# Self attention inside a decoder layer: another order of the same work on GpSimd, VectorE, TensorE, ScalarE and the DMA queue

## The chip, the cores and the metric

The kernel runs on one core of one Trainium2 chip. The metric is the device time of one execution in microseconds (us): TensorE (PE), VectorE (DVE), ScalarE (ACT), GpSimd (POOL) and SyncE (SP), which issues the DMAs of this stage, run their own instruction streams and meet at semaphores.

## The reference, cut to what matters

```
x: (32, 100, 512) float32, 16 heads of 32; ctx: (32, 722, 512)
q, k, v = x@Wq, x@Wk, x@Wv
R_hat   = (1 + exp(v)) / (1 + exp(v - w*|i-j|))           # one 100 x 100 table for each head
scores  = relu(q k^T) * R_hat, causal mask, / sqrt(32)
attn    = softmax(scores);   ctx = attn @ v
x = layernorm(x + ctx @ Wo + bo)
x = layernorm(x + cross_attention(x, ctx_1024))
x = layernorm(x + gated_feed_forward(x))
```

Only the self attention (q, k, v, scores, softmax, attn @ v) is touched. What it computes stays the same.

## The kernel before

The program has three stages in time: self attention (about 0 to 400 us of the trace), a short stage that projects its output, normalises it and projects the queries of the cross attention (400 to 580 us), and cross attention with the feed forward (580 us to the end).

The self attention walks over the 32 batch items b in **steps** s. Two kinds of work are interleaved in a step.

- **Units.** A unit (line 798) is one tile of x@Wq, x@Wk or x@Wv: 12 matmuls, of 320 columns for q and k, of 512 for v. There are 21 for each group of 640 tokens, 105 in all; 11 run ahead of step 0, and each of the first 28 steps holds 3 or 4. In a step they sit in four slots: one unit in each of slots 0, 1 and 2, and the fourth, where there is one, in slot 3. ScalarE takes each from PSUM (`take_unit`, line 528; three PSUM buffers), SP stores it to HBM (`store_unit`), and SP loads q, k and v of item b back as [head dimension, token] tiles (`load_qk`, line 297; `load_v`, line 304).
- **The softmax of one item**, spread over four steps. `scores(b)` (line 821, TensorE) fills one PSUM area; `scale(b)` (655, VectorE) multiplies it with the table into e; `maximum(b, half)` (663) takes row maxima of 8 heads; `exps(b, half)` (541, ScalarE) are eight exponentials with their sums; `invert_sums(b, half)` (670, VectorE) takes 1/sum; `normalise(b, half)` (448, GpSimd) multiplies: the "products"; `turn_blocks(b, half)` (675, VectorE) transposes 32 x 32 blocks of e into the one buffer `turned`. The blocks off the diagonal go from `turned` to `pT` by six DMAs (`move(b)`, line 310, SP), the four on it by four copies (`copy_diagonal(b)`, line 454, GpSimd). `weighted_sum(b)` (831, TensorE) multiplies pT with v, `take_result(b)` (550, ScalarE) takes it from PSUM and `store_o(b)` (322, SP) stores it.

Each engine does its instructions in the order in which they are written; nothing is reordered at run time. `turned` and `pT` are single buffers: `turn_blocks(b)` waits until `move(b-1)` has landed and `copy_diagonal(b-1)` is done, and both of these wait for `weighted_sum(b-1)`. e, q, k, rowsum and the output tile have two buffers or two halves.

In step s, with c = s-1 and b = s-2, the order before is

- TensorE: unit, weighted_sum(s-3), unit, scores(s), unit, and the fourth unit;
- ScalarE: exps(c, 0), unit, exps(c, 1), unit, take_result(s-3), the other units;
- VectorE: scale(c), maximum(c, 0), turn(b, 0), maximum(c, 1), turn(b, 1), invert_sums(c, 0), invert_sums(c, 1);
- GpSimd: products of (c, 0), of (c, 1), copies of b, and in 12 of the steps one eighth of a later token group is split into a high and a low part (`split_x`);
- SP: stores of units, load_qk(s), load_v(s-1), in three steps a load of x, move(s-2), store_o(s-4).

The wait that ties GpSimd's copies to products of the next item stands in `copy_diagonal`:

```
pool.wait_ge(turn_done, 2 * (b + 1))
wait(pool, pv_done, b)
pool.wait_ge(norm_done, 2 * min(b + 2, B))
```

From step 29 on there are no units. There, TensorE does filler matmuls (`between`, line 869), VectorE and ScalarE split the next weights (`c_low`, `c_high`; lines 109 and 103), and the next stage begins on VectorE with `low_o` behind the last `turn_blocks`.

Of the kernel before, what the change touches and what calls it, by code (L numbers as in the profile page):

```python
# [12 lines left out]
KD = D // P  # L13
# [110 lines left out]
def phase_self_attention(nc, sem, passed, xT, wq, wk, wv, w, v, q_d, k_d, v_d, o_d, x, bo, bq, x1_d, cq_d, raws, cross_w,  # L124
# [20 lines left out]
    with ExitStack() as ctx, ExitStack() as of_attention, ExitStack() as of_units, ExitStack() as of_outputs:  # L145
# [123 lines left out]
        with nc.Block() as block:  # L269
# [4 lines left out]
            def _(sp):  # L274
# [3 lines left out]
                def load_x(g):  # L278
                    sp.wait_ge(x_low, 1 + KD * (g - 1))
                    if g == 1:  # L280
                        sp.wait_ge(first_low, KD)
                    sp.dma_start(xraw[:, :, :], x_cols[:, :, col(g * GT, GT)]).then_inc(x_loaded, 16)
# [39 lines left out]
                def store_o(b):  # L322
                    sp.wait_ge(o_done, b + 1)
                    sp.dma_start(tiled[2][:, :, col(b * T, T)], oo[b % 2][:, :, :]).then_inc(o_stored[b % 2], 16)
# [56 lines left out]
                for s in range(B + 3):  # L381
                    while stored < units_before(s):
                        store_unit(stored)
                        stored += 1
                    if s < B:
                        load_qk(s)
                    if 1 <= s < B + 1:
                        load_v(s - 1)
                    if s in (2, 8, 14):
                        load_x((s + 4) // 6 + 1)  # L390
                    if 2 <= s < B + 2:
                        move(s - 2)
                    if s >= 4:
                        store_o(s - 4)
                    if s == LAST_UNITS + 1:
                        sp.wait_ge(unit_done, TOTAL)
                        for which in range(2):
                            for h in range(2):
                                sp.wait_ge(qk_stored[which][h], 16 * NG)
                        for i in range(V_RING):  # L400
                            sp.wait_ge(v_stored[i], 16 * ((TT * NG - i + V_RING - 1) // V_RING))
                        sp.sem_inc(a_freed, 1)
                        load_o(0)
                        load_x1(0)
                        sp.dma_start(bo_b[:, :], bo.rearrange("(a n) -> a n", a=1).broadcast_to([P, D]))\
                          .then_inc(b_loaded, 16)
                        sp.dma_start(bq_c[:, :], bq).then_inc(b_loaded, 16)
# [24 lines left out]
            def _(pool):  # L432
# [6 lines left out]
                def split_x(g, k):  # L439
                    if k == 0:  # L440
                        wait(pool, unit_done, UNITS * (g - 1))
                        pool.wait_ge(x_loaded, 16 * g)
                    pool.tensor_copy(xs[g % 2][0][:, k, :], xraw[:, k, :]).then_inc(x_high, 1)
                    pool.wait_ge(x_high, 2 + KD * (g - 1) + k)
                    pool.tensor_tensor(xs[g % 2][1][:, k, :], xraw[:, k, :], xs[g % 2][0][:, k, :].bitcast(F32),
                                       ALU.subtract).then_inc(x_low, 1)
# [4 lines left out]
                    pool.tensor_tensor(part, part, inv[:, half, :].unsqueeze(2).broadcast_to([T, HH, T]), ALU.mult)\  # L451
                        .then_inc(norm_done, 1)

                def copy_diagonal(b):
                    pool.wait_ge(turn_done, 2 * (b + 1))
                    wait(pool, pv_done, b)

                    pool.wait_ge(norm_done, 2 * min(b + 2, B))
                    for a in range(BLOCKS):
                        rows = slice(32 * a, 32 * (a + 1))  # L460
                        pool.tensor_copy(pT[rows, a, :, :], turned[rows, a, :, :]).then_inc(diag_done, 1)
                    pool.wait_ge(diag_done, BLOCKS * (b + 1))
# [16 lines left out]
                for tile in e:  # L479
# [3 lines left out]
                pool.affine_select(out=rhat[:, :, :], in_=rhat[:, :, :], compare_op=ALU.is_ge, fill=-MASK,  # L483
                                   base=0, pattern=[[0, H], [-1, T]], channel_multiplier=1).then_inc(rhat_done, 1)
                pool.wait_ge(cleared, 3)
                for s in range(1, B + 2):
                    if s <= B:
                        normalise(s - 1, 0)
                        normalise(s - 1, 1)
                    if s >= 2:  # L490
                        copy_diagonal(s - 2)
                    for g in range(2, NG):
                        if 0 <= s - (6 * g - 8) < KD:
                            split_x(g, s - (6 * g - 8))
                pool.wait_ge(b_loaded, 32)
                for g in range(NG):
                    add_bias(g, 0)
# [11 lines left out]
            def _(act):  # L509
# [72 lines left out]
                for s in range(B + 3):  # L582
                    b, c = s - 3, s - 1
                    for i in range(4):
                        if 0 <= c < B and i < 2:
                            exps(c, i)
                        for u in slot(s, i):
                            take_unit(u)
                        if b >= 0 and i == 1:
                            take_result(b)  # L590
                    if s == B - 2:
                        act.wait_ge(a_freed, 1)
                        act.wait_ge(next_loaded, 80)
                        c_high(act, [0])
                    if s == B - 1:
                        for i in range(TT):
                            high_o(0, i)
                    if s == B:
                        c_high(act, [1])
# [14 lines left out]
            def _(dve):  # L614
# [55 lines left out]
                def invert_sums(b, half):  # L670
                    dve.wait_ge(exp_done, H * b + HH * (half + 1))
                    wait(dve, norm_done, 2 * (b - 1) + half + 1)
                    dve.reciprocal(inv[:, half, :], rowsum[:, half, :]).then_inc(inv_done, 1)
# [90 lines left out]
                for s in range(1, B + 2):  # L764
                    b, c = s - 2, s - 1
                    if c < B:
                        scale(c)
                    for half in range(2):
                        if c < B:
                            maximum(c, half)  # L770
                        if b >= 0:
                            turn_blocks(b, half)
                    if c < B:
                        invert_sums(c, 0)
                        invert_sums(c, 1)
                    if s == B - 1:
                        dve.wait_ge(a_freed, 1)
                        dve.wait_ge(next_loaded, 80)
                        c_low(dve, [0])
# [17 lines left out]
            def _(pe):  # L797
# [85 lines left out]
                for s in range(B + 2):  # L883
                    for i in range(4):
                        for u in slot(s, i):
                            unit(u)
                        if s > LAST_UNITS:
                            between(s, i)
                        if i == 0 and s >= 3:
                            weighted_sum(s - 3)  # L890
                        if i == 1 and s < B:
                            scores(s)
                project_o(0, 2)
                weighted_sum(B - 1)
# [1052 lines left out]
```

## Time and profile before

| | us |
|---|---|
| median of 3 runs | 2523.39 (2519.21 to 2528.76) |
| the profiled execution: its own time | 2524.59 |
| the profiled execution: span | 2522.7 |
| mean granted TensorE clock | 0.975 of full speed |
| busy share of the span: PE / DVE / ACT / POOL | 95% / 61% / 53% / 52% |

The busy shares are those of the whole span. In the self attention no engine is busy all the time, and its 400 us have to be read by themselves: by the table of stretches for how full each engine is, and by the order of instructions in time on each engine, with what ended the idle time ahead of each. PE is busy 95% of the span because the cross attention, three quarters of it, fills PE.

### The profile page before, as it was taken

How to read it: one execution, taken by the hardware profiler on the slowest of the kernel's cores; microseconds unless marked ns; L12 is line 12 of the kernel's file. 1: busy time of each engine (PE TensorE's matmuls, PEld its weight loads, DVE VectorE, ACT ScalarE, POOL GpSimd, SP SyncE). 2: the span in 40 equal slices, each digit the busy share in tenths (PEclk: the TensorE clock that was granted, in tenths of full speed). 3: DMA queues.
4: the chain of work that ended last, by engine and by line, in shares of the span. 5: the costliest groups of instructions: out<-in, count | busy, mean ns of one | idle time of the engine just before them, and what ended most of it. 6: DMA issues, size and time to landing. Idle time of an engine off the chain costs nothing.

```text
span 2522.7 us, 58691 instructions
## 1 busy us (share of the span) xinstructions
PE 2396.4 (95%) x21728; PEld 2067.0 (82%) x21728; DVE 1548.0 (61%) x2625; ACT 1326.0 (53%) x3287; POOL 1312.8 (52%) x1125
## 2 busy tenths in 40 slices
PE   7889876997999999999999999999999899999999
PEld 6777744887888888888888888888888688998998
DVE  7556556873766666676666666766666725344342
ACT  4777662213666666666666666666666652321311
POOL 4666545323666656666665656666665523333322
PEclk9999977998999999999999999999999999999999
DMA  6667664743767777777677777776776861011010
GB/s 201 181 195 199 173 188 150 269 155 93 191 180 189 191 187 194 188 190 187 182 190 187 187 191 192 189 186 182 191 188 179 229 187 64 30 34 54 8 38 22
DMA packets 268845, 404.21 MB, mean 160 GB/s; under 512 B 126236, under 2 KB 143644, under 8 KB 268572
## 3 DMA queue, kind: packets, MB, share of 16 engines
q1 hardware_dynamic: 243996, 350.25, 49.0%
q10 hardware_dynamic: 24576, 50.36, 8.3%
q8 instruction: 165, 2.70, 0.5%
q14 instruction: 108, 0.88, 0.1%
HBM read 134.11 MB, written 52.43 MB: 74 GB/s over the span
## 4 chain that ended last, share of the span: by engine, by line
PE 73%; DVE 1%; DMA 1%; SPq 1%; issue 1%; POOL 0%; ACT 0%; POOLq 0%; DVEq 0%; ACTq 0%
PE D_ps_p L68 41%; PE D_ps_s L1748 7%; PE D_ps_p L1774 6%; PE E_ps_u L68 5%; PE E_ps_g L68 5%; PE E_ps_d L68 5%; PE E_ps_y L68 3%; SPq L1198 1%; DMA E_w_int<-in_w_gate 0%; DMA E_x_last<-x 0%; PE E_ps_t L1801 0%; DVE D_neg_max L1557 0%; DVE D_turned L1571 0%; DMA D_values<-in_ctxT 0%; ACT D_e L1421 0%
## 5 line engine op out<-in xcount | busy, mean ns | idle before, releaser
L1305 POOL TENSOR_SCALAR D_e<-D_e,D_inv 128x722 f32<-128x722 f32 x256 | 538.9, 2105 | 538.4 <-DVE D_inv L1563 538.4
L1421 ACT ACTIVATE D_e<-D_ps_s,D_neg_max 128x723 f32<-128x723 f32 x512 | 438.1, 862 | 409.0 <-DVE D_neg_max L1557 358.4
L1557 DVE TENSOR_REDUCE D_neg_max<-D_ps_s 128x1 f32<-128x723 f32 x512 | 439.7, 900 | 313.1 <-PE D_ps_s L1748 312.9
L1571 DVE STREAM_TRANSPOSE D_turned<-D_e 128x768 f32<-128x768 f32 x512 | 496.3, 972 | 7.1 <-DMA D_pT<-D_turned 4.4
L68 PE MATMUL D_ps_p<-D_ctx_high,cross_wk_high 128*128 128x362 f32 (+1 forms) x1024 | 351.0, 343 | 12.4 <-DVE D_ctx_low L1588 12.4
L68 PE MATMUL D_ps_p<-D_ctx_low,cross_wk_high 128*128 128x362 f32 (+1 forms) x1024 | 337.3, 329 | 0.0
L68 PE MATMUL D_ps_p<-D_ctx_high,cross_wk_low 128*128 128x362 f32 (+1 forms) x1024 | 335.9, 328 | 0.0
L68 PE MATMUL D_ps_p<-cross_wv_high,D_ctx_high 128*128 128x512 f32 (+1 forms) x768 | 303.9, 396 | 0.0
L68 PE MATMUL D_ps_p<-cross_wv_high,D_ctx_low 128*128 128x512 f32 (+1 forms) x768 | 303.3, 395 | 0.0
L68 PE MATMUL D_ps_p<-cross_wv_low,D_ctx_high 128*128 128x512 f32 (+1 forms) x768 | 301.7, 393 | 0.0
L1428 ACT ACTIVATE D_e<-D_e,D_inv 128x722 f32<-128x722 f32 x256 | 230.9, 902 | 8.4 <-DVE D_inv L1563 8.4
L68 PEld LDWEIGHTS D_ps_p<-D_ctx_high,cross_wk_high 128*128 128x128 f32 x1024 | 193.3, 189 | 35.1 <-issue 32.3
L547 ACT ACTIVATE A_e<-A_e,A_neg_max 100x100 f32<-100x100 f32 x512 | 185.9, 366 | 51.2 <-DVE A_neg_max L667 50.9
L1320 POOL TENSOR_TENSOR D_ctx_low<-D_craw,D_ctx_high 128x722 fp32r<-128x722 f32 x124 | 198.9, 1604 | 17.4 <-issue 6.9
L1349 POOL TENSOR_TENSOR E_hidden_low<-E_gated,E_hidden_high 128x320 fp32r<-128x320 f32 x120 | 105.4, 880 | 188.6 <-ACT E_hidden_high L1487 188.6
L68 PEld LDWEIGHTS D_ps_p<-D_ctx_low,cross_wk_high 128*128 128x128 f32 x1024 | 194.1, 190 | 2.7
L1748 PE MATMUL D_ps_s<-D_keys,D_queries 32*128 32x241 f32 (+1 forms) x3072 | 193.6, 380 | 2.6 <-ACT D_e L1421 2.6
L68 PEld LDWEIGHTS D_ps_p<-D_ctx_high,cross_wk_low 128*128 128x128 f32 x1024 | 193.8, 189 | 0.0
L1668 DVE SCALAR_TENSOR_TENSOR E_gated<-E_ps_u,E_gated 128x320 f32<-128x320 f32 x120 | 59.0, 492 | 215.2 <-ACT E_gated L1494 215.2
L1748 PEld LDWEIGHTS D_ps_s<-D_keys,D_queries 32*128 32x128 f32 x3072 | 135.1, 185 | 60.8 <-issue 50.5
L68 PEld LDWEIGHTS D_ps_p<-cross_wv_high,D_ctx_low 128*128 128x128 f32 (+1 forms) x768 | 139.1, 181 | 39.6
L1416 ACT ACTIVATE D_values<-D_ps_p 128x512 f32<-128x512 f32 x192 | 114.4, 596 | 106.8 <-PE D_ps_p L68 106.5
(215 smaller groups left out, 5128.0 us busy)
## 6 DMA issues: line engine op xcount, KB each, us to landing
D_pT<-D_turned SPq DMA_DIRECT2D x1536, 96.0 KB, 2.8
D_pT<-D_turned ACTq DMA_DIRECT2D x512, 96.0 KB, 2.9
D_craw<-in_ctxT SPq DMA_DIRECT2D x126, 361.0 KB, 3.8
A_pT<-A_turned SPq DMA_DIRECT2D x192, 64.0 KB, 2.0
self_q<-A_q_out SPq DMA_DIRECT2D x10, 640.0 KB, 3.9
self_k<-A_k_out SPq DMA_DIRECT2D x10, 640.0 KB, 3.9
self_v<-A_v_out SPq DMA_DIRECT2D x25, 256.0 KB, 3.9
A_q<-self_q SPq DMA_DIRECT2D x32, 200.0 KB, 3.9
```

The source lines that it names most:

```text
L68: last = pe.matmul(out, lhs(a, k), rhs(b, k), start=(k == 0 and n == 0), stop=(k == chunks - 1 and n == len(terms) - 1))
L547: act.activation(head, head, ACT.Exp, bias=neg_max[:, b % 2, h:h + 1], accum_out=rowsum[:, half, i:i + 1]).then_inc(exp_done, 1)
L1305: pool.tensor_scalar(head, head, inv[:, 2 * (s % 2):2 * (s % 2) + 1], None, ALU.mult)\
L1320: pool.tensor_tensor(cs[b % 2][1][:, k, :], craw[k % 2][:, :], cs[b % 2][0][:, k, :].bitcast(F32), ALU.subtract).then_inc(c_low, 1)
L1349: pool.tensor_tensor(hs[1][:, c, cols], gated[u % 2][:, :], hs[0][:, c, cols].bitcast(F32), ALU.subtract).then_inc(hl_done, 1)
L1416: act.activation(vs[b % 2][0:rows, i, :], bank("v", b, i)[0:rows, 0:D], ACT.Copy).then_inc(v_done, 1)
L1421: act.activation(e[n // 2 % 2][:, n % 2, 0:PARTS * PART].rearrange("p (a c) -> p a c", a=PARTS), parts_of(n), ACT.Exp, bias=neg_max[:, n % ...
L1428: act.activation(head, head, ACT.Copy, scale=inv[:, 2 * (s % 2) + 1:2 * (s % 2) + 2])\
L1557: dve.tensor_reduce(neg_max[:, n % 4:n % 4 + 1], parts_of(n), AX.XY, ALU.max, negate=True)\
L1571: dve.transpose(turned[quad % 2][:, :, 2 * (s % 2) + h, :].rearrange("p j (t r) -> p t j r", r=32), e[s % 2][:, h, :].rearrange("p (t j r) ...
L1748: return pe.matmul(of_head[:, j, a, 0:end - first], qs[rows, m, :, :].rearrange("p a q -> p (a q)"), ks[rows, m, first:end], start=True, s ...
L1774: last = pe.matmul(out[HD * j:HD * (j + 1), 0:T], vs[b % 2][:, i, c:c + HD], pT[quad % 2][:, :, j, 32 * i:32 * i + QB], start=(i == 0), st ...
```

## The change

Nothing is added but one wait, and nothing removed but the reach of another; instructions change places.

- GpSimd: the four copies of item b now stand ahead of the products of item c = b+1, not behind them; they no longer wait for these products, and wait in addition for those parts of x that GpSimd itself split before (`x_low`, its own finished work).
- VectorE: invert_sums(b, 1) moves from the end of a step to behind the scale of the next one.
- TensorE: weighted_sum and scores each stand one unit later in a step.
- ScalarE: take_result stands behind the unit of slot 2.
- SP: store_o(s-4) stands ahead of move(s-2), not behind it.

```
                     if s in (2, 8, 14):
                         load_x((s + 4) // 6 + 1)
+                    if s >= 4:
+                        store_o(s - 4)
                     if 2 <= s < B + 2:
                         move(s - 2)
-                    if s >= 4:
-                        store_o(s - 4)
...
-                def copy_diagonal(b):
+                def copy_diagonal(b, splits):
                     pool.wait_ge(turn_done, 2 * (b + 1))
                     wait(pool, pv_done, b)
-                    pool.wait_ge(norm_done, 2 * min(b + 2, B))
+                    pool.wait_ge(norm_done, 2 * (b + 1))
+                    pool.wait_ge(x_low, splits)
...
+                splits = 1 + KD
                 for s in range(1, B + 2):
+                    if s >= 2:
+                        copy_diagonal(s - 2, splits)
                     if s <= B:
                         normalise(s - 1, 0)
                         normalise(s - 1, 1)
-                    if s >= 2:
-                        copy_diagonal(s - 2)
                     for g in range(2, NG):
                         if 0 <= s - (6 * g - 8) < KD:
                             split_x(g, s - (6 * g - 8))
+                            splits += 1
...
-                        if b >= 0 and i == 1:
+                        if b >= 0 and i == 2:
                             take_result(b)
...
                     if c < B:
                         scale(c)
+                    if b >= 0:
+                        invert_sums(b, 1)
                     for half in range(2):
...
                     if c < B:
                         invert_sums(c, 0)
-                        invert_sums(c, 1)
...
-                        if i == 0 and s >= 3:
+                        if i == 1 and s >= 3:
                             weighted_sum(s - 3)
-                        if i == 1 and s < B:
+                        if i == 2 and s < B:
                             scores(s)
```

GpSimd in steps 3 and 4. A_e0 and A_e1 are the two buffers of e (items 2 and 3 here), L451 the product of one half, L461 (L462 in the changed kernel) the copies. Before:

```order
L451 TENSOR_TENSOR A_e0<-A_e0,A_inv 100x8x100 [waits A_inv_done,A_diag_done]
L451 TENSOR_TENSOR A_e0<-A_e0,A_inv 100x8x100 [waits A_inv_done]
L461 COPY A_pT<-A_turned 32x512 [waits A_norm_done,A_pv_done,A_turn_done]
L461 COPY A_pT<-A_turned 32x512 x3
L451 TENSOR_TENSOR A_e1<-A_e1,A_inv 100x8x100 [waits A_inv_done,A_diag_done]
```

and now:

```order
L462 COPY A_pT<-A_turned 32x512 [waits A_norm_done,A_x_low,A_pv_done,A_turn_done]
L462 COPY A_pT<-A_turned 32x512 x3
L451 TENSOR_TENSOR A_e0<-A_e0,A_inv 100x8x100 [waits A_inv_done,A_diag_done]
L451 TENSOR_TENSOR A_e0<-A_e0,A_inv 100x8x100 [waits A_inv_done]
L462 COPY A_pT<-A_turned 32x512 [waits A_norm_done,A_x_low,A_pv_done,A_turn_done]
```

The copies of item 1 moved from behind to ahead of both products of item 2.

VectorE in step 3 and at the start of step 4 (L658/L661 is the scale, L667/L670 a maximum, L679/L682 a turn, L673/L676 an inversion). Before:

```order
L658 SCALAR_TENSOR_TENSOR A_e0<-A_ps_s,A_rhat 100x16x100 [waits A_turn_done,A_s_done]
L667 TENSOR_REDUCE A_neg_max<-A_e0 100x8 [waits A_exp_done,A_rel_done]
L679 STREAM_TRANSPOSE A_turned<-A_e1 128x8x4x32 [waits A_diag_done,A_moved,A_norm_done]
L667 TENSOR_REDUCE A_neg_max<-A_e0 100x8 [waits A_exp_done,A_rel_done]
L679 STREAM_TRANSPOSE A_turned<-A_e1 128x8x4x32 [waits A_diag_done,A_moved,A_norm_done]
L673 RECIPROCAL A_inv<-A_rowsum 100x8 [waits A_norm_done,A_exp_done] x2
L658 SCALAR_TENSOR_TENSOR A_e1<-A_ps_s,A_rhat 100x16x100 [waits A_turn_done,A_s_done]
```

and now:

```order
L661 SCALAR_TENSOR_TENSOR A_e0<-A_ps_s,A_rhat 100x16x100 [waits A_turn_done,A_s_done]
L676 RECIPROCAL A_inv<-A_rowsum 100x8 [waits A_norm_done,A_exp_done]
L670 TENSOR_REDUCE A_neg_max<-A_e0 100x8 [waits A_exp_done,A_rel_done]
L682 STREAM_TRANSPOSE A_turned<-A_e1 128x8x4x32 [waits A_diag_done,A_moved,A_norm_done]
L670 TENSOR_REDUCE A_neg_max<-A_e0 100x8 [waits A_exp_done,A_rel_done]
L682 STREAM_TRANSPOSE A_turned<-A_e1 128x8x4x32 [waits A_diag_done,A_moved,A_norm_done]
L676 RECIPROCAL A_inv<-A_rowsum 100x8 [waits A_norm_done,A_exp_done]
L661 SCALAR_TENSOR_TENSOR A_e1<-A_ps_s,A_rhat 100x16x100 [waits A_turn_done,A_s_done]
L676 RECIPROCAL A_inv<-A_rowsum 100x8 [waits A_norm_done,A_exp_done]
```

The second of two inversions in a row moved behind the next scale.

The DMA queue of SP in step 9 and at the start of step 10 (self_o is the stored output, A_q, A_k and A_v the loads of an item, the six A_pT rows one move). Before:

```order
L302 DMA A_q<-self_q 128x4x100 [waits A_q_stored1,A_s_done]
L302 DMA A_k<-self_k 128x4x100 [waits A_k_stored1]
L308 DMA A_v<-self_v 100x512 [waits A_v_stored1,A_pv_done]
L319 DMA A_pT<-A_turned 32x512 [waits A_pv_done,A_turn_done]
L319 DMA A_pT<-A_turned 32x512 x5
L324 DMA self_o<-A_o 128x4x100 [waits A_o_done]
L289 DMA self_v<-A_v_out 128x512 [waits A_unit_out]
```

and now:

```order
L302 DMA A_q<-self_q 128x4x100 [waits A_q_stored1,A_s_done]
L302 DMA A_k<-self_k 128x4x100 [waits A_k_stored1]
L308 DMA A_v<-self_v 100x512 [waits A_v_stored1,A_pv_done]
L324 DMA self_o<-A_o 128x4x100 [waits A_o_done]
L319 DMA A_pT<-A_turned 32x512 [waits A_pv_done,A_turn_done]
L319 DMA A_pT<-A_turned 32x512 x5
L289 DMA self_v<-A_v_out 128x512 [waits A_unit_out]
```

The output's store left the place between a move and the next step's loads.

## Rows read from the trace of the kernel before

**Rows 1.** Table of stretches; columns stretch, length, busy (count) by engine, clock, DMA, GB/s.
```profile
60.00:345.00 285.00, 244.82 (x2722) 212.57 (x2720) 169.53 (x190) 204.98 (x977) 174.83 (x185) 0.96 0.67 186
```

**Rows 2.** Timeline, VectorE, one clean step; start, duration, instruction, [idle before <-releaser].
```profile
219.50 1.25 DVE L679 STREAM_TRANSPOSE A_turned<-A_e 128x1024 f32<-128x1024 f32 x1 [1.79 <-POOL A_pT L461]
220.67 0.94 DVE L667 TENSOR_REDUCE A_neg_max<-A_e 100x8 f32<-100x800 f32 x1
221.54 1.23 DVE L679 STREAM_TRANSPOSE A_turned<-A_e 128x1024 f32<-128x1024 f32 x1
...
224.81 1.78 DVE L658 SCALAR_TENSOR_TENSOR A_e<-A_ps_s,A_rhat 100x1600 f32<-100x1600 f32 x1
...
229.40 1.25 DVE L679 STREAM_TRANSPOSE A_turned<-A_e 128x1024 f32<-128x1024 f32 x1 [1.78 <-POOL A_pT L461]
```

**Rows 3.** Timeline, ScalarE, same step: first and last of eight exponentials.
```profile
221.65 0.38 ACT L547 ACTIVATE A_e<-A_e,A_neg_max 100x100 f32<-100x100 f32 x1 [0.58 <-DVE A_neg_max L667]
...
224.20 0.36 ACT L547 ACTIVATE A_e<-A_e,A_neg_max 100x100 f32<-100x100 f32 x1
```

**Rows 4.** Timeline, GpSimd, the same step: second product, four copies.
```profile
224.97 1.53 POOL L451 TENSOR_TENSOR A_e<-A_e,A_inv 100x800 f32<-100x800 f32 x1 [0.51 <-DVE A_inv L673]
226.66 2.61 POOL L461 COPY A_pT<-A_turned 32x512 f32<-32x512 f32 x4 [0.16 <-POOL A_e L451]
```

**Rows 5.** Waits between 60 and 345 us: total, times, longest.
```profile
DVE A_turned L679 <- POOL A_pT L461: 32.9, 21, 1.8
...
PE A_ps_s L827 <- DMA A_k<-self_k: 21.8, 13, 3.9
```

**Rows 6.** Timeline, VectorE: first turns of items 0, 13, 21 and 27.
```profile
59.99 1.23 DVE L679 STREAM_TRANSPOSE A_turned<-A_e 128x1024 f32<-128x1024 f32 x1
...
199.42 1.25 DVE L679 STREAM_TRANSPOSE A_turned<-A_e 128x1024 f32<-128x1024 f32 x1 [3.25 <-DMA A_pT<-A_turned]
...
283.62 1.25 DVE L679 STREAM_TRANSPOSE A_turned<-A_e 128x1024 f32<-128x1024 f32 x1 [1.79 <-POOL A_pT L461]
...
345.89 1.25 DVE L679 STREAM_TRANSPOSE A_turned<-A_e 128x1024 f32<-128x1024 f32 x1 [0.16 <-POOL A_pT L461]
```

**Rows 7.** DMA issues between 60 and 345 us: count, KB, median us to landing.
```profile
A_pT<-A_turned SPq DMA_DIRECT2D x162, 64.0 KB, 2.0
...
A_k<-self_k SPq DMA_DIRECT2D x26, 200.0 KB, 4.4
```

**Rows 8.** Timeline of SP's queue after the turn of item 17, and the next move.
```profile
243.32 4.59 SPq L319 DMA_DIRECT2D A_pT<-A_turned  x6
247.96 0.58 SPq L324 DMA_DIRECT2D self_o<-A_o  x1
...
249.77 1.31 SPq L302 DMA_DIRECT2D A_k<-self_k  x1
...
253.21 3.68 SPq L319 DMA_DIRECT2D A_pT<-A_turned  x6
```

**Rows 9.** Timeline, TensorE and VectorE: a 320-column unit's first and last matmul, scores(20), scale(20).
```profile
250.94 0.42 PE L68 MATMUL A_ps_a<-A_x_high,A_wk_high 128*128 128x320 f32 x1
...
252.66 0.31 PE L68 MATMUL A_ps_a<-A_x_high,A_wk_low 128*128 128x320 f32 x1
...
255.36 0.96 PE L827 MATMUL A_ps_s<-A_k,A_q 32*100 32x100 f32 x32 [2.39 <-DMA A_k<-self_k]
...
256.39 1.82 DVE L658 SCALAR_TENSOR_TENSOR A_e<-A_ps_s,A_rhat 100x1600 f32<-100x1600 f32 x1 [1.09 <-PE A_ps_s L827]
```

**Rows 10.** Timeline, VectorE: the inversion ahead of scale(1) and of the first turn.
```profile
57.16 0.20 DVE L673 RECIPROCAL A_inv<-A_rowsum 100x8 f32<-100x8 f32 x1 [3.02 <-ACT A_e L547]
```

**Rows 11.** Timeline, TensorE: scores(30).
```profile
366.31 1.01 PE L827 MATMUL A_ps_s<-A_k,A_q 32*100 32x100 f32 x16 [6.39 <-DMA A_k<-self_k]
```

**Rows 12.** Timeline, VectorE: the second turn of item 30, the first of item 31.
```profile
386.31 1.23 DVE L679 STREAM_TRANSPOSE A_turned<-A_e 128x1024 f32<-128x1024 f32 x1
...
395.03 1.25 DVE L679 STREAM_TRANSPOSE A_turned<-A_e 128x1024 f32<-128x1024 f32 x1 [4.50 <-POOL A_pT L461]
```

## What the change was expected to do, written before it ran

> **What bounds the kernel now.** I read the table of stretches first, for the part of the span that the change touches. Between 60 and 345 us, the regular part of the self attention, no engine is full: PE is busy 244.8 of 285 us, DVE 169.5, ACT 205.0, POOL 174.8, and the DMA engines 67% [rows 1]. So waits set this stage, and the step has to be followed in time.
>
> The meter for a step is the distance between the first turns of two items on VectorE. From item 0 (59.99) to item 27 (345.89) it is 285.9 / 27 = 10.59 us [rows 6]. Thirteen of the 27 distances are 9.89 to 9.95 us, the same to a few hundredths, and that is what a closed loop looks like. One of them can be followed through three engines. The turn of item 15 starts at 219.50, the second maximum of item 16 follows 1.17 later [rows 2], the exponentials start 0.98 after that and need 2.91 (221.65 to 224.56) [rows 3], inversion and handoff take 0.41, the product 1.69 to the first copy, the four copies with the handoff 2.74 (226.66 to 229.40) [rows 4], and then the next turn starts, at 229.40 [rows 2]. 1.17 + 0.98 + 2.91 + 0.41 + 1.69 + 2.74 = 9.90. The reader should see why it closes: the copies of item b stand behind the products of item b+1, these need the exponentials of b+1, these the second maximum of b+1, and that stands behind the turn of b. VectorE waits for the copies 21 times here, 32.9 us in all [rows 5].
>
> The other 14 distances are longer. Three hold a load of x (item 13's turn waits 3.25 us for its move [rows 6]), two hold three v units in one step (the turn of item 21 [rows 6]); these five sum to 59.1 us. The remaining 22 sum to 226.8, or 10.31 each; what lengthens them is mostly scores that wait for the load of k, 13 times and 21.8 us in all [rows 5].
>
> **The change, part by part.**
>
> *Copies ahead of the products.* This opens the loop: the copies of b now need only the turn of b and weighted_sum(b-1). What is next? I price every loop that is left, from the same rows.
>
> - Turn and move, through the single buffer: from the first turn's start to the second's end 3.27 us [rows 2], six issues of which the last starts after 5/6 of 3.68 = 3.07 [rows 8], 2.0 to its landing [rows 7], about 0.1 of handoffs: 8.4 us.
> - Turn, copies, first product, turn: 3.27 + 2.61 + 1.53 and three handoffs of 0.13: 7.8 us. The products of the next item are now behind the copies, so they are late only if the copies are; the first product has 8.4 - 7.8 = 0.6 us to spare even in the fastest loop.
> - PE. A 320-column unit takes 252.66 - 250.94 + 0.15 = 1.87 us, scores 0.96 [rows 9], a v unit by its columns 1.6 x 1.87 = 3.0 and a weighted sum about 1.1 (estimates). A step has 105/32 = 3.28 units, 2.50 of them of q and k: 2.50 x 1.87 + 0.78 x 3.0 + 0.96 + 1.1 = 9.1. The busy time agrees: 244.8 us over 285 / 10.59 = 26.9 steps is 9.1 [rows 1].
> - ACT: 205.0 / 26.9 = 7.6 [rows 1]. DVE 6.3, POOL 6.5.
> - SP, over two steps. The loads for scores(s) are issued behind move(s-3), which needs the turn that follows scale(s-2). From scores(s-2) on: 1.03 to the scale, 1.82 for it [rows 9], 0.20 inversion [rows 10], 0.99 maximum, 3.27 turns [rows 2], together 7.3. From there to the next scores but one it was 243.29 to 255.36 = 12.07 [rows 8, 9], where the load of k came last.
>
> *store_o ahead of move.* It takes 0.63 us (247.96 to 248.59) out of exactly this last path [rows 8]. In its new place it needs a result that ScalarE took in the step before, while the queue waits for the turn anyway; what stands behind it is the move. I cost it at nothing, and if take_result were late it would cost the turn's loop what it is late. So the SP loop is (7.3 + 12.07 - 0.63) / 2 = 9.4 with issues as slow as those of rows 8 (4.59 for a move), and some 1.6 less over the two steps, 8.6, where the move takes 3.68 and no unit is stored in between. The rule in the Trainium skill, DMA: Bandwidth & Descriptors, section Queues, rings and completion order, is that descriptors of one issuing engine are consumed in ring order on each DMA engine. By it the 200 KB of store_o no longer go ahead of the load of k either, some tenths more than the issue; I leave these out of the sum.
>
> *inv(b, 1) behind the scale.* It lets scale(c) start without waiting for the last exponentials (VectorE waited 3.02 for them before scale(1) [rows 10]). It puts the second product of b behind scale(c): 0.20 + 0.13 + 1.53 = 1.9 us after the scale, while turn(b, 1) comes 0.20 + 0.99 + 1.17 + 0.87 = 3.2 after it [rows 2, 10]. Cover 1.3 us; a step with a split of x on GpSimd needs 2.3 more only behind that product. Nothing.
>
> *weighted_sum, scores and take_result one unit later.* Between a weighted sum and the next scores stands one unit, as before, so on PE this is a shift by one unit (1.87 us) that is paid once. It is in the sum as part of the start. It has one more effect: the unit of slot 2 is now computed before the scores, so that ScalarE no longer waits for it ahead of the next exponentials. The new x_low wait is for GpSimd's own finished work.
>
> **The sum.** Of the loops left, PE at 9.1 and SP between 8.6 and 9.4 are the longest, two that do not peak in the same steps; I take 9.25 for an ordinary step, near the upper end of SP because every step comes sooner and DMA, now 67% busy, goes to some 76%.
>
> - 22 ordinary steps: 22 x (10.31 - 9.25) = 23.3 us. Bounds: 8.9 gives 31.0; 9.9, as if the old loop had kept its length, gives 9.0.
> - Five steps with a load of x or three v units: these are limited by transfers and by PE, 0.5 each, 2.5 (0 to 5.5).
> - Start: scale(1) need not wait 3.02 us [rows 10], less than the unit that scores come later: 1.5 (0 to 2).
> - End: scores(30) waits 6.39 us for its load behind big loads of the next stage, and that stays but for 0.6 [rows 11]. The last turn waits 4.50 us for copies [rows 12]; the move then comes last, at 386.31 + 1.23 + 5.1 = 392.7, or 2.3 sooner than 395.03, and scale(31) comes sooner since one inversion left its front: 3.5 in all (1 to 5).
>
> 23.3 + 2.5 + 1.5 + 3.5 = 30.8 us off the 2524.6 of the profiled execution: 2493.8. That execution is 1.2 above the median of 2523.4, so 2492.6, rounded **2493**. The later stages start on VectorE behind the last turn and shift as they are.
>
> **Rivals.**
>
> *PE alone, with everything else covered.* Unit work is then all that counts, and steps average 8.9 once the clock stays up: the granted clock is 0.96 in this stretch [rows 1], so some idle time there costs slow matmuls too. 31 + 5.5 + 2 + 4.5 = 43: 2480. For it: loops of 7.8 and 8.4 elsewhere. Against it: 13 waits for k. The Trainium skill, TensorE: Matmul & The Clock Gate, section HAM oscillation, says that idle gaps bring the slow clock back; by it fewer gaps would give this case. 14%.
>
> *The loads take over.* Transfers come denser, the load of k lands 1.0 us later than in rows 8 and comes last in each step: (7.3 + 12.07 - 0.63 + 1.0) / 2 = 9.9, so 9.0 + 0 + 1.5 + 2.5 = 13: 2510. For it: 67% DMA, and k at 4.4 us against 2.0 for a move [rows 7]. 17%.
>
> *The copies keep their time.* Nothing pulls them forward because weighted_sum(b-1) comes last for them and, through the same wait, for the move. Then the turns keep 10.3 and only the end gives something: 4 us, 2519. Against it: their rows show a handoff of 0.16 behind the product, no wait for PE [rows 4]. 8%.
>
> *Slower, by the same queue.* The SP loop passes the old step where (7.3 + L - 0.63) / 2 = 10.59, at L = 14.5 us from the turn's end to scores, so when the load of k lands 2.4 us later than in rows 8 in every step. If it lands 4 us later (denser stores of 640 KB ahead of it), a step is 11.4: 27 x 0.8 = 22 us more, 2545. Nothing shows it in ordinary steps. 4%.
>
> **Numbers.** My forecast, 2485 to 2502, has 57%. A measurement of this kernel tells about 0.5% (12.6 us) from no change, so the edges are 2510.8 and 2536. Faster: 57 + 14 + half of the 17 = 80%. Same: 8 + 8 = 16%, slower 4%. To leave out no more than two in ten, the range takes in the PE case down to 2478 and the loads' case up to 2512.
>
> **What would show it.** Right: first turns 9.1 to 9.4 apart, no regular 9.90, VectorE's wait for the copies near zero; at the end the last turn waits for its move. The waits that replace it: PE for k, or DVE for scores. Wrong: if turns wait for GpSimd's products, the inversion behind the scale was not free; if the move starts late behind store_o, take_result was late; if scores wait for k more than 22 us in all, the loads took over.

## The result, and the profile of the changed kernel

The changed kernel is faster by about 1%, a little less than forecast.

| | before | changed |
|---|---|---|
| median of 4 runs | 2521.3 us (2517.2 to 2528.8) | 2496.9 us (2492.5 to 2497.6) |
| ratio, with its 95% interval | | 0.9896 (0.9869 to 0.9923) |
| profiled execution: own time, span | 2524.6, 2522.7 us | 2492.5, 2490.7 us |

The forecast was 2493, from a median before of 2523.4: 30.8 us less. Measured are 24.4 us less. The profiled execution of the changed kernel is the fastest of its four, so the difference of the two profiles is 32.1 us, and one has to look at where it arises before one calls it the gain of the change.

A step is followed, as before, by the first turn of each item on VectorE. First the turns of items 0, 13 and 27 in the changed kernel (start, duration, instruction, what ended the idle time before):

```profile
58.28 1.23 DVE L682 STREAM_TRANSPOSE A_turned<-A_e 128x1024 f32<-128x1024 f32 x1
...
190.15 1.25 DVE L682 STREAM_TRANSPOSE A_turned<-A_e 128x1024 f32<-128x1024 f32 x1 [4.36 <-DMA A_pT<-A_turned]
...
325.19 1.23 DVE L682 STREAM_TRANSPOSE A_turned<-A_e 128x1024 f32<-128x1024 f32 x1
```

From item 0 to item 27 it is 266.9 us now, 9.89 a step, where [rows 6] had 285.9 and 10.59. The regular 9.90 is gone: in the two traces of before 12 of the 27 distances lie between 9.87 and 9.95 (the prediction counted 13); now 9.86 and 9.87 stand there once each, eleven items apart. The distances now lie between 8.5 and 13.6, seven of them below 9. The shortest, five of 8.52 to 8.60, end in turns that wait for the landed move: that is the loop of turn and move, which the prediction priced at 8.4.

The waits from 60 to 345 us (total, times, longest), which answer to [rows 5]:

```profile
DVE A_e L661 <- PE A_ps_s L831: 80.5, 28, 6.1
...
PE A_ps_s L831 <- DMA A_k<-self_k: 20.8, 15, 2.8
...
DVE A_turned L682 <- DMA A_pT<-A_turned: 18.8, 12, 4.4
...
DVE A_turned L682 <- POOL A_e L451: 2.7, 3, 1.2
```

VectorE's 32.9 us of waiting for GpSimd's copies do not appear any more. In their place VectorE waits 80.5 us for scores, and scores wait for the load of k about as long as before (20.8 us, and 21.8 in [rows 5]). Three turns now wait for GpSimd's products, 2.7 us in all; the prediction had named this as a sign that the moved inversion was not free. The chain can be followed in one step. On VectorE:

```profile
209.76 1.23 DVE L682 STREAM_TRANSPOSE A_turned<-A_e 128x1024 f32<-128x1024 f32 x1
210.92 0.16 DVE L676 RECIPROCAL A_inv<-A_rowsum 100x8 f32<-100x8 f32 x1
214.84 1.82 DVE L661 SCALAR_TENSOR_TENSOR A_e<-A_ps_s,A_rhat 100x1600 f32<-100x1600 f32 x1 [3.76 <-PE A_ps_s L831]
216.58 0.19 DVE L676 RECIPROCAL A_inv<-A_rowsum 100x8 f32<-100x8 f32 x1
```

on TensorE:

```profile
213.80 0.96 PE L831 MATMUL A_ps_s<-A_k,A_q 32*100 32x100 f32 x32 [2.82 <-DMA A_k<-self_k]
```

and in SP's queue ahead of it:

```profile
206.21 0.58 SPq L294 DMA_DIRECT2D self_q<-A_q_out  x1
206.89 0.48 SPq L302 DMA_DIRECT2D A_q<-self_q  x1
207.41 1.17 SPq L302 DMA_DIRECT2D A_k<-self_k  x1
```

VectorE stands idle for 3.76 us until scores are done, scores until the load of k has landed, 6.4 us after its issue at 207.41, behind a 640 KB store of q. The table of stretches has to be read with care here. The stretch of [rows 1], 60 to 345 us, now takes in 20 us of steps without units, where the granted clock was 0.57. Over the same work, from the first turn of item 0 to that of item 27, the rows are, before and now:

```profile
59.99:345.89 285.90, 244.83 (x2722) 212.60 (x2721) 170.26 (x191) 205.11 (x978) 175.53 (x186) 0.96 0.67 186
58.28:325.19 266.91, 243.04 (x2745) 209.56 (x2747) 166.65 (x190) 202.10 (x977) 174.19 (x187) 0.98 0.73 201
```

The engines' work is almost the same and the time is shorter. TensorE is busy 91% of it and not 86%, 9.0 us a step; the DMA share rose from 0.67 to 0.73, and the granted clock from 0.96 to 0.98.

The end of the stage, which answers to [rows 12]: the last turns now wait 2.27 us for the move, not 4.50 for copies.

```profile
368.80 2.37 DVE L682 STREAM_TRANSPOSE A_turned<-A_e 128x1024 f32<-128x1024 f32 x2 [2.27 <-DMA A_pT<-A_turned]
```

To place the gain I split each profile into four parts by turns: up to the first turn of item 0, from there to item 27, from there to item 31, and the rest. The three long steps behind a load of x (to the turns of items 1, 7 and 13) are given apart, and so are the two that the prediction set apart for their v units (to the turns of items 21 and 24; both belong to steps of four units).

| us | to item 0 | 0 to 27 | of it: 3 x, 2 v, each of the other 22 | 27 to 31 | rest of the span |
|---|---|---|---|---|---|
| before | 60.0 | 285.9 | 33.6, 25.6, 10.31 | 49.1 | 2127.7 |
| before, once more | 60.1 | 287.0 | 33.4, 27.0, 10.30 | 49.5 | 2125.6 |
| changed | 58.3 | 266.9 | 38.8, 22.1, 9.36 | 43.6 | 2121.9 |
| changed, once more | 58.7 | 268.9 | 39.4, 21.5, 9.45 | 43.6 | 2126.0 |

The gain of the start does not last. The load of x behind item 0 is issued at the same time as before, 60.66 us after 60.55, so the step to item 1 grew from 11.22 to 13.62, and the turn of item 1 starts no sooner: at 71.21 and 71.55 before, at 71.90 and 71.84 in the changed kernel.

### The profile page after: what moved, and what is told of

It is laid out like the page before. It is cut to its first block, busy times and chain, and to the rows that moved or that the text cites. A ratio compares the mean times of both kernels' runs of the same rounds, so it can differ in the third digit from the quotient of the medians.

```text
span 2490.7 us, 58734 instructions
## 1 busy us (share of the span) xinstructions
PE 2386.9 (96%) x21728; PEld 2057.6 (83%) x21728; DVE 1542.8 (62%) x2625; ACT 1322.3 (53%) x3287; POOL 1309.9 (53%) x1125
## 4 chain that ended last, share of the span: by engine, by line
PE 73%; DVE 1%; issue 1%; DMA 1%; SPq 1%; POOL 1%; ACT 0%; ACTq 0%; DVEq 0%; POOLq 0%
PE D_ps_p L68 41%; PE D_ps_s L1752 7%; PE D_ps_p L1778 6%; PE E_ps_g L68 5%; PE E_ps_u L68 5%; PE E_ps_d L68 5%; PE E_ps_y L68 3%; SPq L1202 1%; DVE D_neg_max L1561 0%; PE E_ps_t L1805 0%; ACT D_e L1425 0%; DVE D_turned L1575 0%; DMA E_w_int<-in_w_gate 0%; DMA D_pT<-D_turned 0%; POOL D_e L1309 0%
```

## Experiments

All are built from the two kernels, and each was timed beside the kernel before on the same chip: e1 to e4 on one (median before 2522.9), e6 to e9 on a second (2523.0), a1, b1 and e5 on a third (2524.2). "Distance" is that from the first turn of item 0 to that of item 27 in the profile.

| run | median us | ratio (95%) | to item 0 | distance | 27 to 31 |
|---|---|---|---|---|---|
| e9_store_only | 2516.5 | 0.9974 (0.9962 to 0.9986) | 59.9 | 284.0 | 48.4 |
| e5_pe_shift_only | 2519.0 | 0.9985 (0.9975 to 0.9996) | 60.4 | 281.4 | 50.1 |
| e1_copies_only | 2515.8 | 0.9967 (0.9951 to 0.9984) | 61.0 | 281.2 | 49.8 |
| e2_copies_inv | 2509.2 | 0.9938 (0.9922 to 0.9955) | 58.7 | 281.7 | 44.8 |
| e3_no_store_move | 2505.4 | 0.9930 (0.9912 to 0.9947) | 59.1 | 277.8 | 45.7 |
| a1_after_again | 2495.8 | 0.9893 (0.9872 to 0.9914) | 58.7 | 268.9 | 43.6 |
| e4_copies_back | 2551.0 | 1.0112 (1.0094 to 1.0130) | 58.8 | 317.4 | 51.2 |
| e6_x_quarters | 2491.5 | 0.9885 (0.9868 to 0.9901) | 59.4 | 261.2 | 43.2 |
| e7_early_qk | 2495.5 | 0.9903 (0.9880 to 0.9925) | 58.4 | 270.9 | 42.4 |
| e8_both | 2496.3 | 0.9905 (0.9885 to 0.9925) | 58.2 | 267.5 | 42.5 |
| b1_before_again | 2524.0 (one run) | | 60.1 | 287.0 | 49.5 |

**How far one profile can be trusted.** This is a second profile of each kernel.

> The changed kernel once more, for a second profile and more times on the chip of the experiments. If the stage lengths read from single profiles carry the argument, the distance from the first turn of item 0 to that of item 27 repeats 266.9 us within about 3 us, and the part behind the last item's turn is 2120 to 2125 us. If they don't repeat, differences of a few us between the experiments say nothing.

> The kernel before once more, one look: the same distance repeats 285.9 us within about 3 us. The part behind the last turn was 2127.7 us in the first profile and 2120 to 2125 in every other; if that was chance it is 2120 to 2126 now, if the old order costs something there it is 2127 again.

The distances repeat within 1.9 and 1.1 us. The rest of the span does not: 2127.7 and 2125.6 for the kernel before, 2121.9 and 2126.0 for the changed one (2120 to 2125 were expected), and 2120.5 to 2124.9 in the nine others. So the 5.8 us that the first two profiles differ by behind the last turn are mostly chance, and the stage itself gave 26.2 us in the first pair (395.03 to 368.80 at the last turn) and 25.5 in the second. The medians differ by 24.4 us in the first pair of timings and by 28.4 in the second (2524.2 and 2495.8), with the stage's own gain between them.

**One edit at a time: the copies.**

```
+                    if s >= 2:
+                        copy_diagonal(s - 2, splits)
                     if s <= B:
                         normalise(s - 1, 0)
                         normalise(s - 1, 1)
-                    if s >= 2:
-                        copy_diagonal(s - 2)
```

The waits in `copy_diagonal` are changed with it, as in the whole change.

> The kernel before with one edit: GpSimd's copies of item b ahead of the products of item b+1. Loop theory (the closed loop of 9.90 us through the copies was what held a step): the loop opens, and the next one is VectorE's own order: both inversions still stand ahead of the next scale, so maximum 0.99, eight exponentials 2.91, a unit 0.42, eight more 2.91, inversion 0.3, scale 1.8, about 9.4 us with handoffs. The first turns of items 0 and 27 are then 270 to 278 us apart (285.9 before, 266.9 in the changed kernel), no distance of 9.90 repeats, ratio about 0.995. Queue theory (scores that wait for k were the true limit, and the other edits brought the gain): 284 to 287 us apart, ratio 1.00.

The distance was 281.2 us, between the two expectations and inside neither: the loop did open (no distance between 9.86 and 9.96 is left, two are below 9), but only 4.7 us of 19 came. VectorE now waits where the loop theory put it, for the exponentials, ahead of the inversion and the scale (waits of 60 to 335 us, in which scores of the kernel before wait 20.7 us for k):

```profile
DVE A_inv L676 <- ACT A_e L550: 86.1, 34, 4.2
...
PE A_ps_s L830 <- DMA A_k<-self_k: 25.9, 15, 3.5
```

**With the inversion behind the scale**, on top of the copies.

```
                         scale(c)
+                    if b >= 0:
+                        invert_sums(b, 1)
...
-                        invert_sums(c, 1)
```

> As the run before, with the second inversion behind the next scale as well. Loop theory: VectorE no longer waits for the last exponentials ahead of a scale; what is left is the place of weighted sum and scores and of the output's store. Turns of items 0 to 27: 268 to 274 us. Queue theory: 284 to 287 us.

The distance stayed, 281.7, inside neither expectation (268 to 274, 284 to 287); 2.3 us came at the start and 5.0 at the end, and the median went 6.6 us down with them. Between items 0 and 27 the wait for exponentials mostly turned into waits for scores (75.2 us), and of these some for k:

```profile
DVE A_e L661 <- PE A_ps_s L831: 75.2, 26, 5.8
...
PE A_ps_s L831 <- DMA A_k<-self_k: 27.6, 17, 3.2
```

**The store left behind the move**, all other edits made.

```
-                    if s >= 4:
-                        store_o(s - 4)
                     if 2 <= s < B + 2:
                         move(s - 2)
+                    if s >= 4:
+                        store_o(s - 4)
```

> The changed kernel with the output's store left behind the move, where it was before. By the two-step loop of SP's queue this puts 0.6 us back between a move and the load of k every step, 0.3 us on a step where that loop is last: 4 to 8 us more than the changed kernel from the first turn of item 0 to that of item 27 (271 to 275 against 266.9), and more wait of scores for k (20.8 us there). Rival: the load of k is hidden elsewhere, then 266 to 268.

The distance was 277.8 us, and scores wait 24.2 us for k instead of 20.8. So the place of one store is worth 8.9 to 10.9 us here, more than the 4 to 8 expected and somewhat more than the 0.63 / 2 x 27 = 8.5 us that it costs if SP's loop is last in every step. It is the largest single share of the gain. This kernel also differs from e2_copies_inv by one edit alone, TensorE's and ScalarE's order: that is worth 3.9 us of distance behind the copies and the inversion.

**The store alone, on the kernel before.**

> The kernel before with one edit: the store of the output ahead of the move. Two loops theory (the loop through the copies and SP's two-step loop both hold steps, and each hides most of what the other gives): the loop of 9.90 us stays, so of the 0.6 us that leave SP's path in every step only those steps profit in which scores waited for k: 2 to 6 us less than 285.9 between the first turns of items 0 and 27, and ratio about 0.998. Rival (the store is worth its 8 to 11 us by itself, as it was behind the other four edits: 277.8 to 266.9): 275 to 278 us.

Here the same edit shortens the distance by 2 to 3 us, as expected, although the wait of scores for k halves, from 20.7 to 9.9 us. The steps of 9.88 to 9.94 become more, 15 instead of 12: the loop through the copies holds them. By the distances the edit is worth 2 to 3 us in one kernel and 9 to 11 in the other, as if two loops of nearly the same length hid each other's gain. The medians do not show this as clearly. By them the store alone gives 6.5 us (2523.0 to 2516.5), and behind the other edits the ratio goes from 0.9930 to 0.9893, about 9 us; with these intervals the two can be equal. That the gain depends on the other edits is likely and not shown.

The edit also has a price, which the prediction put at nothing. The 200 KB of the store now stand between a load of x and the move. In the steps to items 7 and 13 the turn waits 4.3 us for the move in both, not 2.6 and 3.3, and the steps last 12.37 and 12.64 us, where they last 10.69 and 11.64 before (10.71 and 11.22 in the second profile).

**TensorE's and ScalarE's order alone, on the kernel before.**

```
-                        if b >= 0 and i == 1:
+                        if b >= 0 and i == 2:
                             take_result(b)
...
-                        if i == 0 and s >= 3:
+                        if i == 1 and s >= 3:
                             weighted_sum(s - 3)
-                        if i == 1 and s < B:
+                        if i == 2 and s < B:
                             scores(s)
```

> The kernel before with one edit: weighted sum, scores and the taking of the result one unit later. With the loop through the copies still closed (9.90 us), theory: nothing in the regular steps, 283 to 287 us, ratio 0.998 to 1.002, perhaps less wait of ScalarE for units ahead of the exponentials. Rival (scores one unit later lets the load of k land in time): 278 to 282 us.

281.4 us, inside the rival's range; but the load of k is not its way: scores wait for it 18.1 us, hardly less than 20.7. The 22 ordinary steps stay at 10.25, and the two steps to items 21 and 24 go from 25.6 and 27.0 to 20.7. These it eased; that the cause is a unit of v which stood behind the scores and now stands ahead of them is likely and not shown. The ratio is only 0.15% lower. The 4.5 to 5.6 us of distance are about what the same edit gives behind the copies and the inversion (3.9).

**The copies back, all other edits kept.**

> The changed kernel with GpSimd's copies back behind the products of the next item, all other edits kept. Loop theory: the loop closes again, and since the second inversion now stands behind a scale it runs turns 3.3, scale 1.8, inversion 0.3, product 1.6, copies 2.7, about 10.0 us: 282 to 292 us from the first turn of item 0 to that of item 27, all of the gain lost. Queue theory: 266 to 270 us, the gain kept.

The gain was lost, and more: 317.4, outside both expectations, and 28 us slower than the kernel before in the medians. The rows show a loop that I had not seen. On GpSimd:

```profile
222.19 1.52 POOL L451 TENSOR_TENSOR A_e<-A_e,A_inv 100x800 f32<-100x800 f32 x1 [2.28 <-DVE A_inv L673]
223.88 2.60 POOL L461 COPY A_pT<-A_turned 32x512 f32<-32x512 f32 x4 [0.16 <-POOL A_e L451]
```

on TensorE, weighted sum, a unit and scores:

```profile
226.62 1.08 PE L840 MATMUL A_ps_o<-A_pT,A_v 100*32 100x128 f32 x32 [2.79 <-POOL A_pT L461]
...
230.16 0.47 PE L68 MATMUL A_ps_a<-A_x_low,A_wq_high 128*128 128x320 f32 x1
230.42 0.47 PE L68 MATMUL A_ps_a<-A_x_high,A_wq_low 128*128 128x320 f32 x1
230.82 1.23 PE L828 MATMUL A_ps_s<-A_k,A_q 32*100 32x100 f32 x32
```

and on VectorE:

```profile
232.13 1.83 DVE L658 SCALAR_TENSOR_TENSOR A_e<-A_ps_s,A_rhat 100x1600 f32<-100x1600 f32 x1 [2.17 <-PE A_ps_s L828]
233.87 0.19 DVE L673 RECIPROCAL A_inv<-A_rowsum 100x8 f32<-100x8 f32 x1
```

The copies (to 226.48) release the weighted sum, behind it stand a unit and scores, these release the scale, behind that now stands the inversion, and that releases the product at 234.14, behind which stand the next copies (235.82). From copies to copies 11.94 us. With the inversion ahead of the scale, or the copies ahead of the products, this loop does not exist. So the two edits on VectorE and GpSimd belong together, and it is the copies' new place that keeps the moved inversion from costing this much.

**x in quarters**, on the changed kernel. Each of the three later loads of x becomes four of 320 KB, one a step, each ahead of the step's move.

```
-                    if s in (2, 8, 14):
-                        load_x((s + 4) // 6 + 1)
+                    for g in range(2, NG):
+                        if 0 <= s - (6 * g - 10) < KD:
+                            load_x(g, s - (6 * g - 10))
...
```

Each quarter has its own semaphore, and GpSimd waits for it ahead of the split of that quarter.

> The changed kernel with each later load of x cut into four loads of 320 KB, one a step, where one load of 1280 KB stood right ahead of a move. In the changed kernel the three steps behind such a load last 13.62, 12.28 and 12.90 us, and in two of them the turn waited 3.5 and 4.4 us for the landed move. Theory (the move's blocks land behind the bytes of x): these three become 9.5 to 10.5, the nine others get up to 0.5 longer, 258 to 263 us from the first turn of item 0 to that of item 27 (266.9 in the changed kernel). Rival (these steps are long for another reason): no change, 266 to 268.

261.2, inside the expectation. The three steps sum to 30.2 us instead of 38.8 and 39.4. The other 22 are 9.55 instead of 9.36 and 9.45, as the bytes are spread over them. What such a load does in the changed kernel stands in its queue:

```profile
180.01 0.38 SPq L282 DMA_DIRECT2D A_xraw<-in_xT  x1
180.44 0.50 SPq L324 DMA_DIRECT2D self_o<-A_o  x1
181.04 3.72 SPq L319 DMA_DIRECT2D A_pT<-A_turned  x6
```

The move is issued by 184.76, and the turn that waits for it starts at 190.15 with the 4.36 us of idle time shown above; without a load of x ahead the six issues and the landing take about 3.1 + 2.4 = 5.5 us, and not 9.1 (an estimate, from the start of the last issue in this move and the median landing of a block in this trace). The median, 2491.5, is 4 to 5 us under those of the changed kernel (2495.8 and 2496.9, timed apart from it). It is the lowest of all, and clear of the kernel before; against the changed kernel the intervals of the two ratios overlap, so that it beats it is likely and not shown.

**q and k ahead of the move, and both.** SP issues the loads for item s+1 ahead of move(s-2), in the 23 steps in which their units are stored.

```
...
+                    if fetched == s + 1 and ready(s + 1, s):
+                        load_qk(s + 1)
+                        fetched = s + 2
                     if 2 <= s < B + 2:
                         move(s - 2)
```

> The changed kernel with the loads of q and k for item s+1 issued ahead of move(s-2) instead of behind it, in the 23 steps in which the units they need are already stored. Theory (SP's two-step loop, move and then the load of k and then scores, is what holds most steps of the changed kernel): scores no longer wait for k (20.8 us there), and steps go to PE's 9.1: 257 to 263 us for the same distance. Rival (the bytes of q and k now stand ahead of the move's blocks, and the turns wait for the move instead): 266 to 275 us, with VectorE's wait for the landed move above its 18.8 us.

> Both of the two runs before in one kernel. If both causes are real and apart they add up: 249 to 257 us for the distance, ratio about 0.982 to the kernel before. If the bytes ahead of the move are what counts, it is no better than the kernel with quarters of x alone.

270.9 and 267.5: the rival, twice. Together the two edits are no better than the quarters alone (261.2). The waits of e7_early_qk between 60 and 335 us:

```profile
DVE A_e L669 <- PE A_ps_s L839: 62.1, 28, 5.0
...
DVE A_turned L690 <- DMA A_pT<-A_turned: 42.1, 25, 7.1
...
PE A_ps_s L839 <- DMA A_k<-self_k: 12.0, 5, 3.4
```

Scores wait 12.0 us for k instead of 20.8, and turns 42.1 instead of 18.8 for the move: what leads in the queue is early and what follows is late. The load of k is last in many steps of the changed kernel, but issued sooner in this queue it costs the move as much as it gives.

## Why the prediction was right, and where it was not

**The loop of 9.90 us** was read rightly: it is gone with the copies' edit alone. But opening it gave by itself only 4.7 to 5.8 us of distance; the rest of the 18 to 19 came with the other edits, that of the store above all.

**What comes next** was read rightly in the main: SP's two-step loop, which was put between 8.6 and 9.4, with PE at 9.1 (9.0 measured) and turn and move at 8.4 (8.5). That SP's queue sets ordinary steps is shown by the store, whose 0.63 us in the queue are worth 8.9 to 10.9 us; that the load of k alone does is not, since e7_early_qk had it earlier and gained nothing. The 22 ordinary steps measure 9.36 and 9.45 where 9.25 was taken, so this term gave 20.8 and 18.7 us instead of 23.3 (22 times the difference, pair by pair). One step of the 22 holds most of what is missing: the step to item 17 lasts 12.86 us in both profiles of the changed kernel (10.6 and 11.5 before). The other 21 average 9.20 and 9.29. In that step VectorE waits for scores, and these for nothing but TensorE's own work:

```profile
224.92 1.26 POOL L462 COPY A_pT<-A_turned 32x512 f32<-32x512 f32 x2 [4.22 <-PE A_ps_o L843]
...
226.65 0.96 PE L831 MATMUL A_ps_s<-A_k,A_q 32*100 32x100 f32 x32
...
227.68 1.82 DVE L661 SCALAR_TENSOR_TENSOR A_e<-A_ps_s,A_rhat 100x1600 f32<-100x1600 f32 x1 [6.11 <-PE A_ps_s L831]
```

From the scores at 213.80 to those at 226.65 TensorE has no idle time: a unit of k, which falls on the lower level of the clock, and two of v stand ahead of the weighted sum, and one more unit ahead of the scores. GpSimd's copies wait 4.22 us for the same weighted sum. The prediction took TensorE's work by its average over the steps, and here three units in a row are ahead of what the others wait for.

**The five long steps** are the term that was mis-sized: a gain of 2.5 us was forecast, and the three behind a load of x lost 5 to 6 us (33.6 and 33.4 to 38.8 and 39.4). The prediction let them be "limited by transfers", hence no worse. The quarters show that a load of x in one piece is what makes them long: they bring the three from 38.8 and 39.4 down to 30.2. Why they are longer than before is known in part. The step to item 1 is 2.4 and 1.8 us longer, and 1.7 and 1.5 of this are the gain of the start, given back: the load of x is issued when it was before. In the steps to items 7 and 13, the store ahead of the move costs 1.0 to 1.7 us each in e9_store_only; but in e3_no_store_move, where it is back behind the move, they last 12.98 and 12.71 all the same. What lengthens them there stays open. The store's new place, "at nothing" in the prediction, thus had a price in these steps, though not more than it gave in the others. The two steps to items 21 and 24 gained 3.5 and 5.5, so that the five together lost 1.8 and 0.6 us. The prediction gave both three v units; TensorE's rows show three in step 21 and two in step 24.

**Start** 1.5 forecast, 1.7 and 1.5 measured, and lost again by the turn of item 1. **End** 3.5 forecast, 5.5 and 5.9 measured; its mechanism is the one named, and the inversion's place gives most of it (49.8 to 44.8 us between e1 and e2).

Summed by pairs: 20.8 - 1.8 + 1.7 + 5.5 = 26.2 in the first, 18.7 - 0.6 + 1.5 + 5.9 = 25.5 in the second, against 30.8 forecast. The medians say 24.4 and 28.4. Two terms gave less than was forecast and one gave more; that they partly cancel is luck.

**The rivals.** PE alone did not come, though half of its condition did: the granted clock rose from 0.96 to 0.98 and PE's work is 9.0 us a step, but the steps are 9.89 on average, and PE still waits 20.8 us for k. The loads' case did not come either: ordinary steps are 9.4 and not 9.9, and the wait for k stayed just under the 22 us that were to be its sign. The slower case did not come, but the mechanism that would have made this family of edits slower was none of those named: the loop of e4_copies_back, through weighted sum, unit, scores, scale and inversion. The prediction weighed the inversion only by its cover ("Cover 1.3 us"). With the copies ahead that nearly holds: three turns wait for products, 2.7 us in all.

What also stays open: why the distance did not move from e1 to e2. The runs show which wait replaced which, not why the replacement is equally long.

## What to carry to other kernels

A distance that repeats to a few hundredths of a microsecond points to a closed loop: follow it once around by what released each instruction, and price every other loop through the same single buffers before promising more than the next one allows; loops can run over two steps and through a DMA queue. Where two loops are nearly equal, an edit tested alone may look worth less than it is behind the others (2 to 3 us of distance alone and 9 to 11 behind the others here, though the medians leave that open), and one of a pair may be harmful without the other: the moved inversion without the copies' edit made the kernel 28 us slower than before. Compare stretches of the same work, not of the same time: read by a fixed window, the clock here seemed to fall from 0.96 to 0.95, and item by item it rose to 0.98. In a queue that is the last link, what may stand between two urgent transfers is worth more attention than the engines: move or cut large transfers there, and expect that putting one urgent transfer first delays the other.

## What the runs showed of the hardware that was not expected

In these runs a transfer's landing depended on the bytes queued ahead of it more than on its own size: behind 1280 KB of x and 200 KB of the output the six blocks of 64 KB had landed 5.4 us after the end of their last issue, where the median from issue to landing was 2.0 to 2.4 us for one block in the traces of before and of the changed kernel. Cut into 320 KB, the load cost the three steps 9 us less and the 22 ordinary ones together 2 to 4 us more. The Trainium skill, DMA: Bandwidth & Descriptors, section Queues, rings and completion order, has descriptors consumed in ring order on each DMA engine, and these rows agree.

In e4_copies_back a wait of TensorE of 2.79 us was followed, after the weighted sum and the first matmuls of a unit, by matmuls that start 0.27 us apart, at the lower of the clock's two levels (1.2 GHz; the granted clock from 228 to 230 us was 0.51), where they are 0.15 apart at 2.4 GHz [rows 9]; over 200 to 240 us the granted clock was 0.89. The first and the last matmul of that unit start 2.79 us apart (227.63 and 230.42), against 1.72 in [rows 9]. In this loop TensorE's idle time is thus paid a second time, with about 1.1 us of 11.94.
